# Two products in place of three for tiles with one sample, in an expert-routed linear layer

## What is computed

```python
w = L0_cond_weight[itok_B_0_15]                      # (128, 1024, 1024)
y = jnp.einsum('bsi,boi->bso', x, w)
h = jnp.einsum('bsd,nrd->nbsr', y, lora_A)           # 8 adapters of rank 16
lora_out = jnp.einsum('nbsr,nor->bso', h, lora_B * coef)
out = x + jnp.einsum('bsd,od->bso', y, W) + bias + lora_out
```

## Time and profile before

| what | value |
|---|---|
| median of 3 runs | 1508.62 us (1508.57 to 1510.61) |
| the profiled execution, its own time | 1511.33 us |
| its span in the profile | 1509.7 us |
| mean granted TensorE clock | 0.999 |
| PE busy | 1492.8 us (99%) |
| DVE, ACT, POOL busy | 788.1 (52%), 393.2 (26%), 464.4 (31%) us |

### The profile page before, as it was taken

The page is one execution under the profiler, slowest core; times in us unless marked ns, Lnnn a source line. Parts: engine busy times, 40 slices in busy tenths (PEclk is TensorE's granted clock), DMA queues, the critical chain, the costliest instruction groups (busy, mean ns, idle before and its releaser), DMA issues.

```text
span 1509.7 us, 29738 instructions
## 1 busy us (share of the span) xinstructions
PE 1492.8 (99%) x6354; PEld 1190.2 (79%) x6355; DVE 788.1 (52%) x1192; ACT 393.2 (26%) x493; POOL 464.4 (31%) x651
## 2 busy tenths in 40 slices
PE   7999999999999999999999999999999999999998
PEld 4878888888888888878788888888888888888887
DVE  7767766367777368378842333333333333333331
ACT  5244343234444244244430111111111111111110
POOL 4365433533344433534102121221211212212111
PEclk9999999999999999999999999999999999999999
DMA  9979866667787467469744555555555555555553
GB/s 279 293 202 246 221 170 164 186 185 201 202 228 197 142 185 189 156 202 239 192 148 130 142 143 140 136 148 140 133 145 141 138 143 139 144 141 134 146 139 84
DMA packets 172705, 257.90 MB, mean 171 GB/s; under 512 B 31616, under 2 KB 135552, under 8 KB 172672
## 3 DMA queue, kind: packets, MB, share of 16 engines
q1 hardware_dynamic: 128896, 138.62, 36.5%
q10 hardware_dynamic: 23360, 73.28, 16.4%
q0 software_dynamic: 20416, 45.65, 10.9%
HBM read 181.93 MB, written 75.50 MB: 171 GB/s over the span
## 4 chain that ended last, share of the span: by engine, by line
PE 94%; DVE 3%; DMA 1%; ACT 1%; issue 1%; SPq 0%; DVEq 0%; POOL 0%; ACTq 0%; POOLq 0%
PE ps L751 31%; PE ps L755 31%; PE ps L758 31%; DVE w_turn L529 1%; DMA a_sb<-in_L_ffn_lora_A_dram 1%; DMA weff<-fold_sb 1%; DVE w_lo L586 1%; DVE fold_sb L644 1%; DVE x_turn L617 0%; ACT x_hi L409 0%; ACT w_hi L401 0%; PE ps L731 0%; DVE x_lo L624 0%; ACT fold_sb L441 0%; SPq L215 0%
## 5 line engine op out<-in xcount | busy, mean ns | idle before, releaser
L751 PE MATMUL ps<-w_hi,x_hi 128*128 (+1 forms) x2096 | 533.4, 395 | 2.9 <-issue 2.9
L755 PE MATMUL ps<-w_hi,x_lo 128*128 (+1 forms) x2096 | 531.4, 394 | 0.0
L758 PE MATMUL ps<-w_lo,x_hi 128*128 (+1 forms) x2096 | 531.2, 394 | 0.0
L751 PEld LDWEIGHTS ps<-w_hi,x_hi 128*128 128x128 f32 x2096 | 392.8, 188 | 101.8 <-issue 5.4
L755 PEld LDWEIGHTS ps<-w_hi,x_lo 128*128 128x128 f32 x2096 | 392.5, 187 | 97.0
L758 PEld LDWEIGHTS ps<-w_lo,x_hi 128*128 128x128 f32 x2096 | 392.2, 187 | 96.8
L208 POOL DMA_DIRECT2D x_raw<-in_x_dram x560 | 299.1, 534 | 399.8 <-DVE x_turn L617 240.9
L617 DVE STREAM_TRANSPOSE x_turn<-x_raw 128x256 f32<-128x256 f32 x544 | 193.7, 415 | 421.8 <-DMA x_raw<-y_scr 363.8
L409 ACT ACTIVATE x_hi<-x_turn 128x512 fp32r<-128x512 f32 x272 | 166.9, 630 | 686.3 <-DVE x_turn L617 670.6
L384 POOL TENSOR_TENSOR stage<-stage,w_place 128x1024 f32<-128x1024 f32 x64 | 153.1, 2392 | 612.0 <-DMA stage<-in_x_dram 612.0
L624 DVE TENSOR_TENSOR x_lo<-x_turn,x_hi 128x512 fp32r<-128x512 f32 x272 | 180.4, 691 | 128.7 <-ACT x_hi L409 124.2
(11 more groups left out here) (71 smaller groups left out, 40.0 us busy)
## 6 DMA issues: line engine op xcount, KB each, us to landing
w_place<-in_L_cond_weight_dram SPq DMA_DIRECT2D x480, 128.0 KB, 4.4
y_scr<-stage ACTq DMA_DIRECT2D x72, 512.0 KB, 4.3
x_raw<-in_x_dram POOLq DMA_DIRECT2D x560, 64.0 KB, 3.8
x_raw<-y_scr SPq DMA_DIRECT2D x512, 64.0 KB, 2.4
stage<-in_x_dram SPq DMA_DIRECT2D x128, 256.0 KB, 3.7
out_dram<-stage ACTq DMA_DIRECT2D x126, 256.0 KB, 3.0
weff<-fold_sb POOLq DMA_DIRECT2D x8, 512.0 KB, 9.9
w_place<-weff SPq DMA_DIRECT2D x32, 128.0 KB, 3.3
```

What stands on the lines that cost most here:

```text
L751: mm(ps[b][:, cols], x_hi[b][:, t, :], hi[t], start=t == 0, stop=False)
L755: mm(ps[b][:, cols], x_lo[b][:, t, :], hi[t], start=False, stop=False)
L758: last = mm(ps[b][:, cols], x_hi[b][:, t, :], lo[t], start=False, stop=t == KT - 1)
```

## The change

A slot with one sample gets that sample in both positions: a new table `twin`, made with three more small DVE instructions and one more matmul, tells which sample to load at the second. For slots 4 to 63 (`SOLO`), DVE now subtracts each half of x in two instructions. The one for the second position writes to `x_lo` where the slot has a pair, else over the second position in `x_hi`: the tile then holds the rounded sample in its upper 64 rows of the result and its remainder in the lower. PE's new `solo_products` does two passes of 16 matmuls, by `w_hi` and by `w_lo`, and the lower 64 rows of the result are to be added to the upper.

That sum is made at the slots before an expert opens (a slot with one sample is always the last of its expert). ACT copies the whole tile to `stage`, then its lower rows to `low_rows`, which lies in the memory of the first `w_turn`; DVE adds them to the upper rows (`join_y`); where the slot was a pair, DVE writes the sum over `low_rows` itself and `stage` stays. ACT issues the store of that slot after the next expert's weights are rounded. At other slots ACT copies in two halves.

The branch on PE in slots 4 to 63 now reads `slot_used` at the slot's second position: 1 leads to `products`, 0 to `solo_products`. The two matmuls for a slot with no sample stay in slots 1 to 3 and 64 to 71, which are a second loop. ACT and DVE have their slots from 64 and from 61 on written out.

```diff
+    SOLO = range(RING, SAMPLES // 2)
...
+        rows_by = sb("rows_by", [P, (2 + TURN) * D], f32)
+        stage = [rows_by[:, b * D:(b + 1) * D] for b in range(2)]
+        w_turn = [rows_by[:, (2 + b) * D:(3 + b) * D].rearrange("p (t m) -> p t m", m=P) for b in range(TURN)]
+        low_rows = rows_by[0:TOK, 2 * D:3 * D]
...
             def move_y(slot, u, g):
...
+            def move_and_round(slot, u, g):
+                opens = entry(act, slot_opens, 2 * (slot + 1), 1)
+                with act.If(opens > 0):
+                    rank = entry(act, slot_rank, 2 * (slot + 1), EXPERTS - 1)
+                    y_room(slot, u, g)
+                    nc.scalar.activation(stage[u % 2][:, :], ps[u][:, :], COPY)
+
+                    act.wait_ge(w_ready, rank * CHUNKS + CHUNKS)
+                    nc.scalar.activation(low_rows, ps[u][TOK:P, :], COPY).then_inc(copied, 1)
+                    round_w(rank + 1, (rank + 1) % 2)
+                with act.Else():
+                    y_room(slot, u, g)
+                    nc.scalar.activation(stage[u % 2][:, 0:HALF], ps[u][:, 0:HALF], COPY).then_inc(copied, 1)
+                    nc.scalar.activation(stage[u % 2][:, HALF:D], ps[u][:, HALF:D], COPY).then_inc(moved, 1)
+                act.wait_ge(copied, slot - (RING - 1))
+                store_y(slot, u)
...
+            with act.Fori(1, SAMPLES // 2 // RING) as g:
                 for u in range(RING):
                     slot = g * RING + u
-                    round_x(slot + AHEAD, (u + AHEAD) % RING)
+                    round_x(slot + (1 + AHEAD), u)
+                    move_and_round(slot, u, g)
...
-            def turn_x(n, b, raw):
+            def turn_x(n, b, raw, solo):
+
+                pair = entry(dve, slot_used, 2 * n + 1, 1) if solo else None
...
+                    if solo:
+
+                        tt(x_lo[b][:, ts, 0:TOK], x_turn[h][:, :, 0:TOK], x_hi[b][:, ts, 0:TOK], ALU.subtract)
+                        lows = x_both[:, bass.ds(pair + 2 * b, 1), ts, TOK:P].rearrange("p a t m -> p (a t) m")
+                        tt(lows, x_turn[h][:, :, TOK:P], x_hi[b][:, ts, TOK:P], ALU.subtract).then_inc(x_ready, 1)
...
+            def join_y(slot, u):
+
+                dve.wait_ge(copied, slot - RING)
+                pair = entry(dve, slot_used, 2 * slot - 1, 1)
+                tt(rows_by[0:TOK, bass.ds(pair * ((2 - u % 2) * D) + u % 2 * D, D)], ps[u][0:TOK, :],
+                   low_rows, ALU.add).then_inc(moved, 1)
+                dve.wait_ge(moved, slot)
+
+            def prepare_next_expert(slot, joined=None):
                 opens = entry(dve, slot_opens, 2 * slot, 1)
                 with dve.If(opens > 0):
+                    if joined is not None:
+                        join_y(slot, joined)
...
+            def solo_products(b, par, n, ready):
+
+                pe.wait_ge(x_ready, n * 2 + 2)
+                for half in range(2):
+                    cols = slice(half * HALF, (half + 1) * HALF)
...
+                    pe.wait_ge(w_rounded, ready + (half + 1) * CHUNKS // 2)
+                    for t in range(KT):
+                        mm(ps[b][:, cols], x_hi[b][:, t, :], hi[t], start=t == 0, stop=False)
+                    pe.wait_ge(w_ready, ready + (half + 1) * CHUNKS // 2)
+                    for t in range(KT):
+                        last = mm(ps[b][:, cols], x_hi[b][:, t, :], lo[t], start=False, stop=t == KT - 1)
+                last.then_inc(tile_done, 1)
+
+            def run_pair_or_solo(slot, u):
+                pair = entry(pe, slot_used, 2 * slot + 1, 1)
+                with pe.If(pair > 0):
...
+                    products(u, rank % 2, slot, rank * CHUNKS)
+                with pe.Else():
...
+                    solo_products(u, rank % 2, slot, rank * CHUNKS)
...
-            with pe.Fori(1, SLOTS // RING) as g:
+            with pe.Fori(1, SAMPLES // 2 // RING) as g:
+                for u in range(RING):
+                    slot = g * RING + u
+                    pe.wait_ge(moved, slot - (RING - 1))
+                    run_pair_or_solo(slot, u)
+            with pe.Fori(SAMPLES // 2 // RING, SLOTS // RING) as g:
                 for u in range(RING):
                     slot = g * RING + u
                     pe.wait_ge(moved, slot - (RING - 1))
                     run_slot(slot, u)
```

More of the change, by code:

```diff
@@ L132, in grouped_adaln_ffn_kernel @@
         n_ranks = sb("n_ranks", [1, 1], i32)
+        twin = sb("twin", [1, SLOTS], i32)
+        alone = scratch("alone", [1, SLOTS], f32)
+        own = scratch("own", [1, SLOTS], f32)
         slot_sample, slot_rank, slot_opens, slot_used = [slot_tab[i:i + 1, :] for i in range(4)]
@@ L199, in load_sample @@
         def load_sample(eng, n, b, h, loaded, quads=range(QUADS)):
-            sample = entry(eng, slot_sample, 2 * n + h, SAMPLES - 1)
-            if not (isinstance(n, int) and n < RING):
+            late = not (isinstance(n, int) and n < RING)
+            sample = entry(eng, *((twin, n) if late and h else (slot_sample, 2 * n + h)), SAMPLES - 1)
+            if late:
                 eng.wait_ge(x_turned, 2 * n - (2 * RING - 2))
@@ L420, in round_next_expert, with y_room @@
                     act.nop()
-            def move_y(slot, u, g):
+            def y_room(slot, u, g):
                 act.wait_ge(tile_done, slot + 1)
@@ L426, in move_y, with store_y @@
                     act.wait_ge(stored[u % 2], g * (16 * RING // 2) + 16 * (u // 2))
-                nc.scalar.activation(stage[u % 2][:, :], ps[u][:, :], COPY).then_inc(moved, 1)
+            def store_y(slot, u):
                 act.wait_ge(moved, slot + 1)
@@ L470, in _ @@
                 move_y(slot, slot, 0)
-            with act.Fori(1, SLOTS // RING) as g:
+            round_x(RING + AHEAD, AHEAD)
+            round_next_expert(RING)
+            with act.Fori(1, SAMPLES // 2 // RING) as g:
                 for u in range(RING):
                     slot = g * RING + u
-                    round_x(slot + AHEAD, (u + AHEAD) % RING)
+                    round_x(slot + (1 + AHEAD), u)
+                    move_and_round(slot, u, g)
+            for slot in range(SAMPLES // 2, SLOTS):
+                if slot > SAMPLES // 2:
+                    round_x(slot + AHEAD, (slot + AHEAD) % RING)
                     round_next_expert(slot)
-                    move_y(slot, u, g)
+                move_y(slot, slot % RING, slot // RING)
             def out_step(g, u, last):
@@ L594, in prepare_w, with prepare_x @@
                 split_w(k, par, chunks[-1])
[L596 removed]
+            def prepare_x(n, b, raw, load, loaded=x_loaded, loads=QUADS, solo=False):
                 for sems in loaded:
                     dve.wait_ge(sems[raw], load * (16 * loads) + 16 * loads)
[L600 removed]
+                turn_x(n, b, raw, solo)
             def prepare_first(n):
@@ L635, in x_index @@
                 return n // RING - (1 if n % RING else 2)
+            pairs = slot_sample.rearrange("a (n h) -> a h n", h=2)
+            link(tt(own[:, :], alone[:, :], pairs[:, 0, :], ALU.mult))
+            tt(twin[:, :], own[:, :], pairs[:, 1, :], ALU.add).then_inc(tables, 1)
             prepare_w(0, 0, range(0, CHUNKS // 2))
```

44 lines of the change are left out of this document (27 added, 17 removed).

## The result

The changed kernel takes **1526.47 us** (median of 6 runs, 1523.37 to 1530.54) against 1509.61 for the kernel before (6 runs, 1508.4 to 1512.74). The ratio is 1.0105, with a 95% interval of 1.0094 to 1.0117: 16.9 us slower, where +1.8 us was forecast with a range up to 1516. The profiled execution took 1528.75 us with a span of 1527.1, that is 17.4 us more than the span before.

The account below looks back on a forecast made before the run. The prediction took PE, 99% busy, as the bound. Matmuls +0.77 us, a wait at slot 5 +0.5 and cold code at slot 66 +0.5 made +1.8 on 1508.62: 1510.4 us, range 1507.4 to 1516.

Parts of the forecast that it names:

- 0.2333 us a matmul: PE's price per matmul, from 8 matmuls taking 1.867 us on the timeline; a tile with 48 costs 11.20 us.
- six singles at -3.73: Six one-sample slots (10, 14, 23, 35, 38, 44) take two passes, not three: 3.73 us less each, 22.40 in all.
- the four empty slots that take the long way: Empty slots 5, 28, 49, 59 get 32 matmuls, 7.47 us each, in place of two: 23.17 us more in all.
- The net +0.77 us: PE's matmul sum over slots 4 to 63: -22.40 us for one-sample slots and +23.17 for empty ones.
- slot 5's old hole: At empty slot 5 PE lost 4.92 us, mostly at low clock; the 32 matmuls cover it, costing 2.55 us more.
- its new wait, put at 0.5 us: PE waits at slot 5 for the later x from DVE: 0.5 us, ends 0 and 2.0.
- The step that failed: ACT's half copies and later store at expert openings cost nothing, with ACT busy for 26% and three PSUM tiles ahead.
- 8.4 us left at slot 36: At slot 36 the next expert's weights had 8.4 us to spare: 20.15 us of work, ready at 408.54, slot starting 416.9.
- this remainder covers 2.2 us: Where an expert opens, ACT's second copy and DVE's sum, 2.2 us ahead of the weights, cost nothing within 8.4 us spare.
- DVE becomes the pace at the short experts: Slower rival: at experts 7 and 8 DVE loses 2.4 to 7.0 us each, a 4.9 us hole, 1515.3 us; chance 0.14.
- Cold code at slot 66: Slower rival: empty slot 66 comes in PE's new second loop, 4.3 us more in place of 0.5, 1514.2 us; chance 0.12.
- Refetched code: Slower rival: longer loop bodies no longer stay loaded, PE pauses once a turn, 6 us, 1516.5 at least; chance 0.05.

Follow-up runs that it names:

- PE's part ran alone: Kernel before with only PE's part of the change (two passes in slots 4 to 63, slots 64 to 71 a second loop): 1512.81 us, ratio 1.0016.
- the last runs: Changed kernel, ACT moving first: empty slots short, sum only behind singles, by table reads 1554.95 us, by a start-made table 1496.33; or 24 DVE loop instructions added, 1553.27.
- the kernel with the two more table reads: Changed kernel, ACT moving first, empty slots on two matmuls, copy and sum only behind a single, by two more table reads: 1554.95 us, ratio 1.0299.
- the one by a table: Changed kernel, ACT moving first, empty slots on two matmuls, copy and sum only behind a single, by a table made at the start: 1496.33 us.
- the two kernels with short empty slots: Changed kernel with empty slots on two matmuls again, 1521.74 us; the same with ACT's move also ahead of rounding the next x, 1502.86 us.

## Why the prediction was wrong

**Right.** PE is the bound; 0.2333 us a matmul; six singles at -3.73; the four empty slots that take the long way. The net +0.77 us showed as +1.2 in the span (1510.9 against 1509.7) when PE's part ran alone, where the timed ratio gives +2.4 (1.1 to 3.9); what the 1.6 us above the sum are, no run shows. The empty slots in the range measured 7.47 us each (slot 5, just behind its wait, 7.56), slot 5's old hole with its low clock was covered as forecast, and its new wait, put at 0.5 us, was 0.8.

**The step that failed** is the one on ACT: "The two copies of a half each at other slots, and the later store of one slot at each expert, are on ACT, busy for 26%, with three more PSUM tiles ahead of PE: nothing." It costed what ACT does, not where it stands. The change also moves the rounding of x ahead of the move from PSUM, which the text did not price at all. I looked for cover in one place, the weights (8.4 us left at slot 36), and the weights never were late for PE. The cover that mattered was that of the PSUM tile: in the kernel before, the move of slot 6 ends at 129.08 + 1.01 = 130.1, PE's sequencer would need some 2.7 us more (as measured in the change), and slot 10 starts at 136.45, so 3.6 us were left. PE itself came to the end of slot 9 later by 4.0 us (140.38), which adds to them. But that move now ends 11.5 us later, at 141.56. Of these the order makes 4.6 (5.5 us from the last weights to the move's end, where it was 0.9), the opening 4.0 (5.2 in place of 1.2; I had 2.2 for it, the durations without the table reads and hand-overs between them), and the x of slot 9, itself later and longer, the other 2.9 or so. 11.5 less 3.6 and 4.0 is the hole of 3.9. The time of PE's sequencer stands on both sides of this sum, so the sum does not check it.

A second term failed with it: "I cost the copy and the sum at nothing, because this remainder covers 2.2 us". They took 4.0 us at the opening, and without them the kernel is 13.3 us faster, because they make the same move late.

**The rivals.** "DVE becomes the pace at the short experts" was near in kind: the holes of slots 40 and 43 stand right behind experts 7 and 8, and DVE's lag from one expert passes to the next. ACT's last roundings of the weights prepared at slots 33, 36 and 39 end at 414.3, 452.0 and 490.1, where they ended at 407.2, 441.0 and 474.5: 7.1, 11.0 and 15.6 us late, a loss of 3.9 and 4.6 us per short expert, inside the 2.4 to 7.0 that the rival gave. But its mechanism was late weights, and what came late was the release of PSUM; its price of 4.9 us for a hole with slow clock was near for each of three holes (5.6, 4.6, 4.0). Cold code at slot 66: 0.56 us when PE's part ran alone, so the term of 0.5 us in the sum was nothing, and the 2.5 us more in the changed kernel are put down to ACT's move. Refetched code: not in the changed kernel, whose packets are 30. The Trainium skill, page "Runtime: NRT & Kernel Launch", section "Instruction fetch mechanics", told of a stall at jumps outside the loaded pages; the last runs agree in kind: 24 instructions more in DVE's loop than this kernel has bring the stalls. They came on DVE, not on PE's jumps.

**The range.** It took one hole at a time. Three long ones came together, since they have one cause.

## What to carry to other kernels

When an edit changes the order of an engine that frees a buffer, compute for each buffer, at its tightest use, when it is freed and when it is wanted, with the time of the waiting engine's own sequencer; a busy share of 26% says nothing about it. A branch that asks a narrower question than the old one sends the remaining cases somewhere: count them (here four empty slots ate the gain of six singles). And look at the instruction queues after any edit to a loop: a body that no longer stays loaded costs far more than its instructions (here 39 us for 24 of them).

## What the hardware showed that was not expected

- A loop body on DVE of 284 or 288 instructions was loaded once; 308 were loaded in every turn, 96 packets in place of 32, and cost 39 us over the 14 turns (1513.98 to 1553.27), though four of the six instructions added for each slot were executed once at most. Where exactly the limit lies, and how it depends on the place of the body in the program, was not tried.
- In the changed kernel the granted clock fell after each of the three holes of 2.5 to 4 us, some 1.6 us lost each time, and not after the hole of 1.1 us. The length of the hole alone does not decide it. In the kernel with the two more table reads PE started again at 192.64 after a hole of 3.4 us, and the clock stayed at 1.00; in the one by a table the hole ahead of slot 60 was 2.1 us, and the clock of the stretch behind it was 0.64. No run here shows what decides. The first of the two, PE and its stretch:

```profile
192.64 2.13 PE L825 MATMUL ps<-w_hi,x_both 128*128 x8 [3.20 <-ACT x_both L419]
```

```profile
192.60:198.00 5.40, 5.36 (x23) 4.38 (x24) 0.83 (x3) 1.11 (x3) 4.16 (x8) 1.00 1.07 293
```

- A wait of PE that ends late costs 2.1 to 3.1 us more until the first matmul in the changed kernel, where two table reads and a branch follow it. The same code took 3.6 us at slot 10 of two other kernels (without the sum, and with the whole subtraction), and 4.2 and 4.3 us with a third table read in the two kernels with short empty slots. When the wait is early, all of it is hidden.
